# A rope tail shared out differently between VectorE and GpSimd, and minus-maxima turned by one transpose and sent as two rows

## The chip, the cores and the metric

The kernel runs on 1 core of one Trainium2 chip. The metric is the device time of one execution in microseconds; the number given for a kernel is the median of its runs. TensorE does the matrix products, VectorE, ScalarE and GpSimd do elementwise work (the profile calls them PE, DVE, ACT and POOL), and SyncE and ScalarE issue the DMA transfers. An engine executes its own list of instructions in order; engines wait for one another by semaphores.

## The reference

Two layers are computed on x of shape (2, 512, 512), so T = 1024 tokens, D = 512, everything in float32.

```
xn = layernorm(x)
x  = x + attention0(xn) + ffn0(xn)      # 32 query heads, 8 key/value heads, head size 16, rope, causal softmax, w_o
                                        # ffn: silu(xn Wg') * (xn Wu') Wd', 1792 wide, W' = W * (su @ sv), rank 4
xn = layernorm(x)
x  = x + attention1(xn) + ffn1(xn)      # 4 heads, tanh-like weights; ffn 1376 wide with rank-16 additions
```

In attention0 each query head takes 16 columns of xn @ w_qkv, is turned by the rope tables (x1 cos - x2 sin, x1 sin + x2 cos), and its scores are scaled by 1/4, masked and put through a softmax.

## The kernel before, in words

**Products in three passes.** A float32 operand is split into a rounded part "hi" (ScalarE copies it into fp32r) and the rest "lo" (a subtraction, mostly on GpSimd). `three_pass` (L50 to L54) then makes hi*hi + lo*hi + hi*lo, three matmuls of 128x512 each for one 128-row slice.

**The qkv stage** (`qkv_stage`, L449). SyncE loads the eight 128-token tiles of x (four before `w_qkv`, four after it, L489), the weights and tables. Tiles 0 to 3 are normalised (`Norm`, L64), transposed on TensorE and split. GpSimd subtracts the low halves of the weights (L521, then four chunks, L524). Six "pairs" (batch, k) of products follow in the order of `pairs` (L477): keys and two halves of the queries of batch 0, then of batch 1. For pair n, VectorE multiplies by cos and sin (L611, four instructions), GpSimd adds and subtracts into `rope_sum` (L538, L540), ScalarE makes `rope_hi` (L579), GpSimd makes `rope_lo` in `rest(n)` (L531), and SyncE stores all to DRAM (`store_pair`, L504), from where `load_stack` brings the stacked operands of a group back. In its iteration n GpSimd runs `rest(n - 1)`, and after the loop `rest(5)`. Buffers alternate with n % 2, so ScalarE waits for the store of pair n - 2 before it overwrites them. Tiles 4 to 7 are normalised meanwhile and transposed behind pairs 0 and 1.

**The attention stage** (`attention_stage`, L759) interleaves the first feed-forward layer with the attention by hand. A step is one `three_pass` of a gate or up product; 16 steps make one of 14 chunks (`Up`, L145): steps 0 to 7 work on batch 0, steps 8 to 15 on batch 1. For a chunk, VectorE combines the factor product and the raw weight (L206), ScalarE and GpSimd split it (L215, L219), ScalarE takes tanh of the gate product (L281), VectorE makes `up_gated` (L288) and `hidden` (L296). TensorE may not start step 8 before `up_gated` of batch 0. The right factors of all chunks are split in four parts at steps given by `LR0_HI_AT` (ScalarE, L920) and `LR0_LO_AT` (VectorE, L137). Every instruction of an engine stands in the order of the steps.

After every third step from 18 on stands a burst of attention work; four bursts (k = 0 to 3) make one group of 4 query heads, 16 groups in all. In a group, TensorE makes scores for the row maxima (L1003), VectorE reduces them (L949) and negates two query blocks at a time (L959), `minus_max` transposes the 128x4 result of each of the two blocks (L1011), ScalarE copies the 4x256 rows out of PSUM (L890) and issues one DMA (L896) that puts them into the last row of `q_stack`, so that the second score product (`key_scores`, L1025, one burst round later) already holds score minus maximum. Query blocks 3 and 2 ("high") are turned in burst k = 3, blocks 1 and 0 ("low") in burst k = 1 of the next group. ScalarE then takes exp (L903), GpSimd masks the diagonal blocks (L868), and `values` (L1038) at k = 0 multiplies by v once all four diagonal blocks of its group are masked. `key_scores` of the first piece waits for the high rows, the piece (0, 1), the last of burst k = 2, for the low rows.

**The down stage** (`down0_stage`, L1081, with `DownBehindUp`, L394) has 14 chunks of 12 matmuls per batch. Its VectorE loop makes, for each chunk o, `down_w_eff` (L348), `down_w_lo` (L357), and beside them the reciprocals of the softmax sums (L1231, for o = 6 to 9) and their low half (L1236). Its ScalarE loop makes `down_w_hi` three chunks ahead (L353), then `down_h_hi` two chunks ahead (L367), the split of w_o (L1190) and of the attention result (L1185). GpSimd makes `down_h_lo` (L372), and after those of batch 0 and the first two of batch 1 `att_lo` (L1172), which TensorE needs right behind chunk 13.

## Time and profile before

| | |
|---|---|
| median of 3 runs | 744.0 us (743.83 to 745.27) |
| the profiled execution | 743.73 us, of which 742.0 us are the span of the trace |
| busy in the span | TensorE 698.9 us, VectorE 413.2, ScalarE 289.4, GpSimd 246.0 |
| TensorE's mean granted clock | 0.975 of full speed |

The working is made on the profiled execution: its span and 1.7 us around it. That execution lies 0.3 us below the median. A matmul of 128x512 follows the one before it after about 0.23 us at full clock; the duration that a row prints for it is longer, since matmuls overlap. "idle before <-X" is the time for which the engine had nothing to execute before this instruction, and what ended it.

### The profile page before, as it was taken

To read this page: it belongs to the slowest core of one execution; us is meant where nothing else is said; L and a number is where in the kernel's file an instruction comes from. 1 tells how busy PE (TensorE), PEld (TensorE's weight loads), DVE (VectorE), ACT (ScalarE), POOL (GpSimd) and SP (SyncE) were. 2 spreads that over 40 slices of the span, in tenths; PEclk is the share of its full clock that TensorE was granted. 3 is DMA by queue.
4 is the path that set the end of the run, shared out by engine and by line. 5 is a ranking of instruction groups with operands and counts; after the bars stand their busy time and mean duration, and the time that the engine had idled before them with its cause. 6 is when DMAs were issued, how large, how long until landed. Compare 5 with 4: busy or idle time off the path is not lost. (4 is left out here: it accounts for less than half of the span.)

```text
span 742.0 us, 10322 instructions
## 1 busy us (share of the span) xinstructions
PE 698.9 (94%) x3718; PEld 530.4 (71%) x3718; DVE 413.2 (56%) x980; ACT 289.4 (39%) x541; POOL 246.0 (33%) x246
## 2 busy tenths in 40 slices
PE   8996999999989999999999799879999999997998
PEld 6875766666656665666677588667888888875886
DVE  7653676767766756675475550386444554535611
ACT  4214145545544534455434222263333333323321
POOL 4677122222322312221434345133232332202443
PEclk9999999999999999999999999969999999998999
DMA  9337802432231225102256200110000100102211
GB/s 289 122 110 179 209 3 71 100 80 73 70 71 47 55 41 111 42 30 72 83 167 206 89 15 1 48 58 29 29 29 30 49 37 1 41 0 86 71 57 57
DMA packets 23163, 54.88 MB, mean 74 GB/s; under 512 B 3780, under 2 KB 4136, under 8 KB 22056
## 3 DMA queue, kind: packets, MB, share of 16 engines
q1 hardware_dynamic: 22856, 54.08, 26.1%
q8 instruction: 30, 0.49, 0.3%
q14 instruction: 21, 0.17, 0.1%
q10 hardware_dynamic: 256, 0.13, 0.1%
HBM read 42.53 MB, written 11.54 MB: 73 GB/s over the span
## 5 line engine op out<-in xcount | busy, mean ns | idle before, releaser
L949 DVE CUSTOM_DVE_ANT_0 bank<-bank,mask 128x512 f32<-128x512 f32 (+3 forms) x256 | 118.4, 523 | 71.8 <-PE bank L1003 71.6
L219 POOL TENSOR_TENSOR up_w_lo<-up_w_eff,up_w_hi 128x512 fp32r<-128x512 f32 x50 | 67.2, 1352 | 120.4 <-ACT up_w_hi L215 120.4
L52 PE MATMUL bank<-x0T_hi,up_w_hi 128*128 128x512 f32 x224 | 97.4, 435 | 6.7 <-DVE up_gated L288 5.9
L372 POOL TENSOR_TENSOR down_h_lo<-hidden,down_h_hi 128x512 fp32r<-128x512 f32 x50 | 64.7, 1294 | 100.4 <-ACT down_h_hi L367 100.4
L903 ACT ACTIVATE probs<-bank 128x512 f32<-128x512 f32 x160 | 85.4, 598 | 32.1 <-PE bank L1025 29.5
L54 PE MATMUL bank<-x0T_lo,up_w_hi 128*128 128x512 f32 x224 | 90.2, 403 | 0.0
L53 PE MATMUL bank<-x0T_hi,up_w_lo 128*128 128x512 f32 x224 | 90.1, 402 | 0.0
L868 POOL TENSOR_SCALAR_AFFINE_SELECT probs<-probs 128x512 f32<-128x512 f32 x64 | 39.9, 635 | 133.3 <-ACT probs L903 133.3
L52 PE MATMUL bank<-down_w_hi,down_h_hi 128*128 128x512 f32 x200 | 79.4, 397 | 3.2 <-POOL down_h_lo L372 2.1
L53 PE MATMUL bank<-down_w_hi,down_h_lo 128*128 128x512 f32 x200 | 78.7, 394 | 0.0
L54 PE MATMUL bank<-down_w_lo,down_h_hi 128*128 128x512 f32 x200 | 78.6, 393 | 0.0
L52 PE MATMUL bank<-x1T_hi,up_w_hi 128*128 128x512 f32 x176 | 73.2, 416 | 3.6 <-DVE hidden L296 3.2
L54 PE MATMUL bank<-x1T_lo,up_w_hi 128*128 128x512 f32 x176 | 69.4, 395 | 0.0
L53 PE MATMUL bank<-x1T_hi,up_w_lo 128*128 128x512 f32 x176 | 69.4, 394 | 0.0
L52 PEld LDWEIGHTS bank<-x0T_hi,up_w_hi 128*128 128x128 f32 x224 | 42.8, 191 | 30.0 <-issue 15.5
L1025 PE MATMUL bank<-q_stack,k_stack 49*128 49x512 f32 x160 | 58.2, 447 | 5.6 <-DMA q_stack<-minus_max_rows 5.6
L367 ACT ACTIVATE down_h_hi<-hidden 128x512 fp32r<-128x512 f32 x50 | 31.5, 630 | 80.3 <-PE bank L54 76.6
L288 DVE SCALAR_TENSOR_TENSOR up_gated<-up_tanh,bank 128x512 f32<-128x512 f32 x50 | 34.2, 684 | 50.1 <-ACT up_tanh L281 50.1
L1003 PE MATMUL bank<-k_stack,q_stack 48*128 48x512 f32 (+3 forms) x256 | 57.5, 344 | 0.0
L296 DVE SCALAR_TENSOR_TENSOR hidden<-up_gated,bank 128x512 f32<-128x512 f32 x50 | 34.3, 685 | 39.0 <-PE bank L54 38.8
L215 ACT ACTIVATE up_w_hi<-up_w_eff 128x512 fp32r<-128x512 f32 x50 | 31.2, 631 | 54.4 <-DVE up_w_eff L206 54.3
L54 PEld LDWEIGHTS bank<-x0T_lo,up_w_hi 128*128 128x128 f32 x224 | 43.2, 193 | 10.6
(142 smaller groups left out, 1332.1 us busy)
## 6 DMA issues: line engine op xcount, KB each, us to landing
w_raw<-in_w_gate_up SPq DMA_DIRECT2D x25, 512.0 KB, 4.0
w_raw<-in_w_down SPq DMA_DIRECT2D x25, 256.0 KB, 2.8
q_stack<-q_hi SPq DMA_DIRECT2D x32, 128.0 KB, 4.0
att<-att_T SPq DMA_DIRECT2D x16, 256.0 KB, 2.0
x<-in_x SPq DMA_DIRECT2D x8, 256.0 KB, 5.4
q_hi<-rope_hi SPq DMA_DIRECT2D x8, 256.0 KB
q_lo<-rope_lo SPq DMA_DIRECT2D x8, 256.0 KB
q_stack<-q_lo SPq DMA_DIRECT2D x16, 128.0 KB, 4.1
```

Of the source, the lines that this page charges most:

```text
L52: pe.matmul(out, w_hi, m_hi, start=first, stop=False, skip_group_check=True)
L53: pe.matmul(out, w_lo, m_hi, start=False, stop=False, skip_group_check=True)
L54: return pe.matmul(out, w_hi, m_lo, start=False, stop=last, skip_group_check=True)
L219: pool.tensor_tensor(self.half(self.w_lo[:, o % 2], k), self.half(self.w_eff, k), f32(self.half(self.w_hi[:, o % 2], k)), ALU.subtract).th ...
L288: dve.scalar_tensor_tensor(out=self.ut[:, b, :], in0=self.th[:, b, :], scalar=1.0, in1=self.product_bank(o, b, 0)[:, :], op0=ALU.add, op1= ...
L296: dve.scalar_tensor_tensor(out=self.hid[:, o, b * S:(b + 1) * S], in0=self.ut[:, b, :], scalar=0.5, in1=self.product_bank(o, b, 1)[:, :], ...
L372: pool.tensor_tensor(self.h_lo[:, k % 2, :], self.hid[:, o, b * S:(b + 1) * S], f32(self.h_hi[:, k % 2, :]), ALU.subtract).then_inc(self.h ...
L868: pool.affine_select(out=diag, in_=diag, compare_op=ALU.is_ge, fill=0.0, base=0, pattern=[[0, REP], [1, P]], channel_multiplier=-1).then_i ...
L903: act.activation(pt[:, BLOCK_OF[KEY_PIECES[p]], :, :], narrow.bank(("keys", g, p))[:, :].rearrange("p (h s) -> p h s", h=REP), ACT.Exp).th ...
L949: dve.tensor_tensor_reduce(out=own, in0=own, in1=e.mask[:, S - w:S], scale=1.0, scalar=NEG, op0=ALU.add, op1=ALU.max, accum_out=rmax[:, i, ...
L1003: last = pe.matmul(bank[:, n * w:(n + 1) * w], qst[K, slot, h + n, i * P:(i + 1) * P], kst[K, slot, 0:w], start=(n == 0), stop=(n == nh - ...
L1025: pe.matmul(narrow.bank(("keys", g, p))[:, :], kst[K, slot, j * P:(j + 1) * P], qst[K, slot, :, i * P:(i + 1) * P], start=True, stop=True) ...
```

## The change

Three places are edited.

1. **Qkv stage.** The four second tiles of x come in one DMA. VectorE takes the statistics of tiles 4 to 7 first, then subtracts the low half of the last weight chunk (which GpSimd did), then normalises the four tiles; ScalarE's four square roots stand behind its four weight copies. `rest(3)`, `rest(4)` and `rest(5)` move from GpSimd to VectorE: behind the products of pairs 4 and 5 and behind the loop. The four parts of the right factors are split at steps 6, 8, 10, 12 (hi) and 7, 9, 11, 13 (lo), where it was 1, 6, 9, 14 and 2, 7, 10, 15.
2. **Attention stage.** `minus_max` turns two query blocks with one transpose of 128x8 to 8x128. ScalarE copies 8x128 where it copied 4x256, and issues two DMAs of four rows of 128 for each half of a group, 64 in all where there were 32. The waits of `key_scores` ask for both.
3. **Down stage.** `down_w_lo` stands behind the reciprocals and their low half. On ScalarE the first two parts of w_o are split one chunk earlier, and so are the first two parts of the attention result.

```diff
@@ -461,14 +461,14 @@
         prod = sb("rope_products", [P, 2, 4, S])
...
         cos, sin = e.cos, e.sin
-        x_loaded = [sem(f"x_loaded{t}") for t in range(NT)]
+        x_loaded = [sem(f"x_loaded{t}") for t in range(NJ)] + [sem("x_second_batch_loaded")] * NJ
         norm = Norm(nc, ctx, "norm0", x_sb, x_sb, lambda t: (x_loaded[t], 16), lambda t: e.bank[4 + (t if t < NJ else t % 2)], e.ident,
...
         lr_lo, products, stored = e.lr0_lo, e.rope_products, e.rope_stored
-        w_hi_ready, w_lo_ready = sem("wqkv_hi_ready"), sem("wqkv_lo_ready")
+        w_hi_ready, w_lo_ready, w_lo_last = sem("wqkv_hi_ready"), sem("wqkv_lo_ready"), sem("wqkv_lo_last_ready")
         v_mm, v_ones = sem("v_mm"), sem("v_ones")
@@ -485,8 +485,7 @@
                 sp.dma_start(x_sb[:, t, :], d["x"][t * P:(t + 1) * P, :]).then_inc(x_loaded[t], 16)
...
                 sp.dma_start(w_raw[:, c, :], d["w_qkv"][c * P:(c + 1) * P, :]).then_inc(w_loaded[c], 16)
-            for t in range(NJ, NT):
-                sp.dma_start(x_sb[:, t, :], d["x"][t * P:(t + 1) * P, :]).then_inc(x_loaded[t], 16)
+            sp.dma_start(x_sb[:, NJ:, :], d["x"][S:].rearrange("(t p) n -> p t n", p=P)).then_inc(x_loaded[NJ], 16)
             sp.dma_start(cos[:, :], d["cos"]).then_inc(consts, 16)
...
             sp.dma_start(lr_raw[:, :], d["lr0"]).then_inc(lr_in, 16)
@@ -519,7 +518,7 @@
                 pool.memset(e.v[:, b], 1.0).then_inc(v_ones, 1)
...
             pool.tensor_tensor(w_lo[:, :, 0:P], w_raw[:, :, 0:P], f32(w_hi[:, :, 0:P]), ALU.subtract).then_inc(w_lo_ready, 1)
-            for c in range(NC):
+            for c in range(NC - 1):
                 pool.wait_ge(w_hi_ready, c + 2)
@@ -539,7 +538,7 @@
                                    ALU.subtract).then_inc(summed, 1)
...
                                    ALU.add).then_inc(summed, 1)
-                if n >= 1:
+                if 1 <= n <= 3:
                     rest(n - 1)
...
                     pool.wait_ge(lo_ready, 2)
@@ -547,8 +546,6 @@
                 if n == 4:
...
                         up.pool_lo(pool, 0, k)
-            rest(len(pairs) - 1)
-
         def scalar(act):
...
                 for c in range(NC):
@@ -566,7 +563,8 @@
             norm.act_hi(act, 3)
...
                 act.activation(w_hi[:, c, P:], w_raw[:, c, P:], ACT.Copy).then_inc(w_hi_ready, 1)
-                norm.act_std(act, NJ + c)
+            for t in range(NJ, NT):
+                norm.act_std(act, t)
             act.wait_ge(v_ones, B)
...
                 for t in HI_BEFORE.get(n, ()):
@@ -594,12 +592,19 @@
             norm.dve_norm(dve, NJ - 1)
...
                 norm.dve_lo(dve, t)
-            norm.dve_stats(dve, NJ)
-            for t in range(NJ + 1, NT):
+            for t in range(NJ, NT):
                 norm.dve_stats(dve, t)
-                norm.dve_norm(dve, t - 1)
-            norm.dve_norm(dve, NT - 1)
+            dve.wait_ge(w_hi_ready, NC + 1)
+            dve.tensor_tensor(w_lo[:, NC - 1, P:], w_raw[:, NC - 1, P:], f32(w_hi[:, NC - 1, P:]), ALU.subtract).then_inc(w_lo_last, 1)
+            for t in range(NJ, NT):
+                norm.dve_norm(dve, t)
             dve.wait_ge(consts, 32)
+
+            def rest(n):
+                R = rows[pairs[n][1]]
+                dve.wait_ge(hi_ready, n + 1)
+                dve.wait_ge(lo_ready, n)
+                dve.tensor_tensor(rot_lo[0:R, n % 2], rot[0:R, n % 2], f32(rot_hi[0:R, n % 2]), ALU.subtract).then_inc(lo_ready, 1)
...
                 dve.wait_ge(pair_mm, n + 1)
@@ -615,9 +620,12 @@
                     norm.dve_lo(dve, t)
...
                     stack_lo(dve, e.lr0, lr_raw, slice(0, D), slice(D, LR0_FIRST), lr_hi, 1, lr_lo)
+                if n >= 4:
+                    rest(n - 1)
                 if n == 4:
...
                         up.dve_combine(dve, 0, k)
+            rest(len(pairs) - 1)
...
             pe.wait_ge(e.ident_in, 16)
@@ -633,8 +641,10 @@
                     for r in range(2):
...
                         for c in range(NC):
-                            if (n, r) == (1, 0):
+                            if (n, r) == (1, 0) and c < NC - 1:
                                 pe.wait_ge(w_lo_ready, c + 2)
+                            if (n, r) == (1, 0) and c == NC - 1:
+                                pe.wait_ge(w_lo_last, 1)
                             last = three_pass(pe, e.bank[2 * (n % 2) + r][0:rows[k], :], w_hi[:, c, c0:c0 + rows[k]],
...
                                               e.xT_lo[:, c, b * S:(b + 1) * S], c == 0, c == NC - 1)
@@ -748,7 +758,7 @@
...
 LR0_REST = [slice(LR0_FIRST + 6 * n * P, LR0_FIRST + 6 * (n + 1) * P) for n in range(4)]
-LR0_HI_AT, LR0_LO_AT = {1: 0, 6: 1, 9: 2, 14: 3}, {2: 0, 7: 1, 10: 2, 15: 3}
+LR0_HI_AT, LR0_LO_AT = {6: 0, 8: 1, 10: 2, 12: 3}, {7: 0, 9: 1, 11: 2, 13: 3}
 LRD0_PARTS = [slice(CH0 * P, CH0 * P + D)] + [slice(448 * n, 448 * (n + 1)) for n in range(4)]
...
 DOWN_FACTOR = {211: 0, 214: 1, 217: 2}
@@ -768,7 +778,7 @@
         att = sb("att_T", [P, 2, S])
...
         negm = sb("minus_max", [P, NJ, REP])
-        negrow = sb("minus_max_rows", [REP, NJ, P], F32R)
+        negrow = sb("minus_max_rows", [2 * REP, 2, P], F32R)
         lrd_raw = e.hid[0:96, 10:13, :].rearrange("p o t -> p (o t)")[:, 0:CH0 * P + D]
...
         ones = sem("k_ones")
@@ -885,16 +895,15 @@
                 r, slot = rows_of(g)
...
                 if g >= 1:
-                    act.wait_ge(neg_row[half], 16 * g)
-                both = slice(2 * half, 2 * half + 2)
-                act.activation(negrow[:, both, :],
-                               narrow.bank(("minus_max", g, half))[0:REP, 0:2 * P].rearrange("h (i s) -> h i s", i=2),
-                               ACT.Copy).then_inc(neg_copied, 1)
+                    act.wait_ge(neg_row[half], 32 * g)
+                act.activation(negrow[:, half, :], narrow.bank(("minus_max", g, half))[0:2 * REP, 0:P], ACT.Copy).then_inc(neg_copied, 1)
                 act.wait_ge(neg_copied, 2 * g + 2 - half)
...
                     act.wait_ge(s2_mm, KEYS * (g - 3))
-                act.dma_start(f32(qst[r + STK - 1:r + STK, slot, :, 2 * half * P:2 * (half + 1) * P]),
-                              f32(negrow[:, both, :])).then_inc(neg_row[half], 16)
+                for n in (1, 0):
+                    i = 2 * half + n
+                    act.dma_start(f32(qst[r + STK - 1:r + STK, slot, :, i * P:(i + 1) * P]),
+                                  f32(negrow[n * REP:(n + 1) * REP, half, :])).then_inc(neg_row[half], 16)
...
                 act.wait_ge(s2_mm, KEYS * g + p + 1)
@@ -1007,19 +1016,17 @@
             def minus_max(g, half):
...
                 narrow.free(pe, ("minus_max", g, half))
-                for i in range(2):
-                    last = pe.transpose(narrow.bank(("minus_max", g, half))[0:REP, i * P:(i + 1) * P],
-                                        negm[:, 2 * half + i, :], e.ident[:, :])
-                last.then_inc(neg_mm, 1)
+                pe.transpose(narrow.bank(("minus_max", g, half))[0:2 * REP, 0:P],
+                             negm[:, 2 * half:2 * half + 2, :].rearrange("p i h -> p (i h)"), e.ident[:, :]).then_inc(neg_mm, 1)
...
                 if p == 0:
-                    pe.wait_ge(neg_row[1], 16 * (g + 1))
+                    pe.wait_ge(neg_row[1], 32 * (g + 1))
                 if (j, i) == (0, 1):
-                    pe.wait_ge(neg_row[0], 16 * (g + 1))
+                    pe.wait_ge(neg_row[0], 32 * (g + 1))
                 narrow.free(pe, ("keys", g, p))
...
                 pe.matmul(narrow.bank(("keys", g, p))[:, :], kst[K, slot, j * P:(j + 1) * P], qst[K, slot, :, i * P:(i + 1) * P],
@@ -1200,11 +1207,17 @@
                     b = (o - 5) // 2
...
                     act.activation(rden[0:2 * HEADS, b, :], den[:, b, :], ACT.Copy).then_inc(rden_hi, 1)
+                if o == CH0 - 3:
+                    wo_half(0)
+                    wo_half(1)
                 down.act_hhi(act, (o + 2) // CH0, (o + 2) % CH0)
-                if o >= CH0 - 2:
-                    wo_half(2 * (o - CH0 + 2))
-                    wo_half(2 * (o - CH0 + 2) + 1)
-            for c in range(NC):
+                if o == CH0 - 3:
+                    att_half(0)
+                if o == CH0 - 2:
+                    wo_half(2)
+                    wo_half(3)
+                    att_half(1)
+            for c in range(2, NC):
                 att_half(c)
...
                 down.act_hhi(act, 1, o)
@@ -1223,7 +1236,6 @@
...
                 down.dve_combine(dve, o)
-                down.dve_wlo(dve, o)
                 if 6 <= o < 10:
...
                     if o == 6:
@@ -1234,6 +1246,7 @@
                     low = slice(HEADS, 2 * HEADS)
...
                     dve.tensor_tensor(rden[low, b, :], den[low, b, :], f32(rden[low, b, :]), ALU.subtract).then_inc(rden_s, 1)
+                down.dve_wlo(dve, o)
                 if o >= CH0 - 3:
```

## Rows read from the trace of the kernel before

**Rows 1.** What TensorE waited for: us in total, times, longest
```profile
PE bank L52 <- DVE up_gated L288: 5.9, 1, 5.9
PE bank L1025 <- DMA q_stack<-minus_max_rows: 5.6, 4, 1.9
...
PE bank L52 <- POOL att_lo L1172: 3.8, 1, 3.8
...
PE bank L52 <- POOL down_h_lo L372: 2.1, 3, 0.9
```

**Rows 2.** Timeline, rope tail: start us, us, engine, line, operation, idle before
```profile
56.80 1.06 ACT L579 ACTIVATE rope_hi<-rope_sum 128x1024 fp32r<-128x1024 f32 x1 [6.15 <-DMA q_lo<-rope_lo]
58.46 2.51 POOL L219 TENSOR_TENSOR up_w_lo<-up_w_eff,up_w_hi 128x512 fp32r<-128x512 f32 x2 [1.99 <-ACT up_w_hi L215]
61.02 0.51 PE L52 MATMUL bank<-x0T_hi,up_w_hi 128*128 128x512 f32 x1 [0.82 <-POOL up_w_lo L219]
63.42 4.73 POOL L531 TENSOR_TENSOR rope_lo<-rope_sum,rope_hi 128x1024 fp32r<-128x1024 f32 x2
66.32 2.65 DVE L137 TENSOR_TENSOR lr<-lr_raw,lr 32x768 fp32r<-32x768 f32 x1 [5.34 <-ACT lr L920]
73.02 0.95 DVE L137 TENSOR_TENSOR lr<-lr_raw,lr 32x768 fp32r<-32x768 f32 x1
73.04 0.79 PE L52 MATMUL bank<-x0T_hi,up_w_hi 128*128 128x512 f32 x1 [5.92 <-DVE up_gated L288]
```

**Rows 3.** Line L489's loads of x tiles 4 to 7
```profile
L489 SPq DMA_DIRECT2D x<-in_x x4: 554/568/667, 5.0 to 7.0; - x4
...
DMA to landing us min/median/max: 6.7/6.8/6.8
```

**Rows 4.** Line L100, all eight: duration ns min/median/max, first and last start
```profile
L100 DVE TENSOR_SCALAR x<-x,norm_mv,norm_rstd x8: 545/548/1918, 5.9 to 20.3; 128x512 f32<-128x512 f32 x8
```

**Rows 5.** Timeline, qkv stage, GpSimd, VectorE and TensorE
```profile
13.12 4.94 POOL L524 TENSOR_TENSOR wqkv_lo<-wqkv_raw,wqkv_hi 128x640 fp32r<-128x640 f32 x3
14.71 1.92 DVE L100 TENSOR_SCALAR x<-x,norm_mv,norm_rstd 128x512 f32<-128x512 f32 x1
18.89 1.03 PE L108 MATMUL bank<-ident,x 128*128 128x128 f32 x8
```

**Rows 6.** Windows: stretch, length, busy of PE, PEld, DVE, ACT, POOL, granted clock, DMA
```profile
73.00:76.00 3.00, 2.96 (x7) 2.38 (x8) 2.58 (x3) 0.72 (x1) 0.00 (x0) 0.50 0.58 161
```

**Rows 7.** Timeline, TensorE, one burst with a transpose pair
```profile
99.30 0.38 PE L1011 MATMUL bank<-ident,minus_max 128*4 128x128 f32 x2
99.61 0.49 PE L1003 MATMUL bank<-k_stack,q_stack 48*128 48x512 f32 x1
```

**Rows 8.** Lines of `minus_max_rows`, ScalarE: duration ns min/median/max
```profile
L890 ACT ACTIVATE minus_max_rows<-bank x32: 355/373/374, 92.9 to 350.4; 4x256 fp32r<-4x256 f32 x32
L896 ACTq DMA_DIRECT2D q_stack<-minus_max_rows x32: 580/581/1178, 93.3 to 350.8; - x32
```

**Rows 9.** Timeline, last masks of a group and its value products, groups 0 and 1
```profile
108.65 1.22 POOL L868 TENSOR_SCALAR_AFFINE_SELECT probs<-probs 128x512 f32<-128x512 f32 x2 [2.28 <-ACT probs L903]
110.20 2.36 PE L1038 MATMUL bank<-probs,v_ones 128*32 128x512 f32 x32
125.23 1.22 POOL L868 TENSOR_SCALAR_AFFINE_SELECT probs<-probs 128x512 f32<-128x512 f32 x2 [0.24 <-ACT probs L903]
126.50 2.36 PE L1038 MATMUL bank<-probs,v_ones 128*32 128x512 f32 x32
```

**Rows 10.** Timeline, TensorE, the longest of its four waits for a row transfer
```profile
219.65 0.50 PE L1025 MATMUL bank<-q_stack,k_stack 49*128 49x512 f32 x1 [1.90 <-DMA q_stack<-minus_max_rows]
```

**Rows 11.** Timeline, down stage, VectorE, TensorE, GpSimd
```profile
376.04 1.74 DVE L1231 RECIPROCAL den_or_left_factors<-den_or_left_factors 64x256 f32<-64x256 f32 x1
385.03 0.50 PE L52 MATMUL bank<-down_w_hi,down_h_hi 128*128 128x512 f32 x1 [0.72 <-POOL down_h_lo L372]
411.19 2.62 POOL L1172 TENSOR_TENSOR att_lo<-attention_or_xn,att_hi 128x512 fp32r<-128x512 f32 x2 [0.29 <-ACT att_hi L1185]
```

## Prediction

> **What bounds the kernel now.** I read TensorE's row of waits first. It has the most work, and the chain that ended last runs through its matmuls, so a microsecond counts only if TensorE idles less, executes less, or runs at a higher clock. Four of its waits lie where this change works [rows 1]: 5.9 us once for `up_gated`, 5.6 us in four waits for row transfers, 3.8 us once for `att_lo`, 2.1 us in three for `down_h_lo`. Next I read the timeline ahead of each, by engine, and last the granted clock behind the longest.
>
> **Rope tail, what it gains.** Before, GpSimd ends the sums of pair 5 at 63.4, then subtracts `rope_lo` twice, 4.73 us. VectorE wants the right factors at 66.32 and needs 2.65 us for what takes 0.95 us alone [rows 2]: it stood still until GpSimd's subtraction ended at 68.15. Behind it come the second combine, ScalarE's split, its table load, tanh, `up_gated`, and TensorE restarts at 73.04. From the end of that subtraction, 68.97, this takes 4.07 us.
>
> After: `rest(4)` waits for `rope_hi` of pair 4, which is held by the store of pair 2 until 56.80 as before, and ends at 57.86. VectorE subtracts 128x1024 then, from 57.9; by the 0.95 us for 768 elements that is 1.2 us, to 59.1. GpSimd wanted to start `up_w_lo` at 58.46. The two have just been seen not to run side by side, so it starts at 59.1, 0.6 us late, and TensorE's start at 61.02 becomes 61.6 (bounds: 0, if GpSimd is first and VectorE waits, to 1.2). Queued behind it are the sums of pair 5, at 64.1 instead of 63.4, then `rope_hi`, 1.06 us, `rest(5)` on VectorE, 1.2 us with GpSimd idle, to 66.4. Both combines follow at once, for no factor split stands between them now; the second ends 0.6 us behind the first, so at 67.0 VectorE is where it was at 68.97, and the 4.07 us give a restart at 71.0 to 71.1. Gain 2.0 us, less what comes next.
>
> **First quarter, what it costs.** The last of four loads was issued at 7.0 and landed 6.7 us later [rows 3]; queued bytes are the same, so one load lands at about 13.7, 0.8 us after VectorE wants tile 4. Four statistics of 0.8 us end at 16.9. The weight subtraction then meets GpSimd's three, which end at 18.06 (17.8 without today's mutual waits), as L100 met the first of them, 1.92 us against 0.55 [rows 4, 5]. So it runs to 18.5, tiles 4 and 5 are normalised at 19.2 and 19.9 (0.13 us of reciprocal and 0.55 each), and TensorE, which transposed both from 18.89 [rows 5], starts pair 1 some 0.6 us later. From below 0, if the subtraction slips in between two of GpSimd's; from above 1.4, if its block is 0.8 us longer. TensorE has no other wait until 60, so the 0.6 us carries through. `rest(3)` runs beside the sums of pair 4 and delays them by up to 1.2 us, hidden behind the store that lands at 56.8. SyncE's stores and stack loads come earlier, and with three issues fewer at the start so do the loads queued behind x; nobody waits for those. The split parts, moved by steps, fit in ScalarE's and VectorE's idle time before step 16 (the third takes 0.95 us of VectorE; if the cover were gone, 1 us). Net: restart 1.4 us earlier.
>
> **Clock.** Behind the 5.9 us TensorE ran at 0.50, the level of 1.2 GHz [rows 6], for a while, and some ten matmuls took 0.43 us each for 0.23: 2 us. The wait is now near 3.4 us. The one of 3.8 us [rows 1] is the nearest; behind it the half-clock stretch cost about 1.3 us. I take 1.1 us, so 0.9 us is given back; bounds 0 and 2. **Rope tail in all: -2.3 us**, between -4 and 0.
>
> **Transposes, what they gain.** Two transposes and the change of tile to the next product take 0.31 us [rows 7]; the eight transposes of x take 1.03 us with the end of the last [rows 5], so one costs 0.10 to 0.13 us, and 0.105 fits both. 32 fewer: -3.4 us, all of it TensorE's own work (bounds -3.2 and -4.1). The 8x128 copy saves ScalarE 128 elements per partition, 0.11 us of 0.37.
>
> **The second row transfer, what it costs.** ScalarE's issue takes 0.58 us [rows 8] and about 0.04 us to the next; ScalarE does nothing else in it. Queued behind are, at k = 3, the last two exps, then GpSimd's two masks, then `values`. Net of the shorter copy they come 0.51 us later. How near is this already? Of 16 groups, in six the masks end 0.33 us before the value products (109.87 and 110.20 [rows 9]), in four 0.05 us before (126.45 and 126.50), which is no slack at all, and in six over 0.5 us. The products can start 0.04 us after the mask. So six waits of 0.23 us and four of 0.5 to 0.6 us, one of which hides in a longer wait: 1.4 + 1.7 + a little for the copy's start, +3.3 us. If the short pattern issues in half the time, 0.3 us, only the four remain, with +1.0 us; I take 3.0.
>
> The rows themselves: the low half must be there at the last piece of burst k = 2, some 3.5 us after its issue, and TensorE waited already four times, up to 1.90 us [rows 10]. The second transfer leaves 0.51 us later against a TensorE that comes 0.1 us earlier. If it lands so much later, the four waits grow by 2.4 us and a few that just fitted by 1.2; if it lands with the first, because both stand behind the same bulk loads, by nothing. Middle, 1.8, and 0.7 for one more half-clock stretch. **Attention in all: -3.4 + 3.0 + 1.8 + 0.7 = +2.1 us**, between -2.4 and +6.
>
> The Trainium skill speaks against the edit: "DMA: Bandwidth & Descriptors", Rules for kernel authors, says that two transfers to disjoint partition halves serialise, since both use the same engines, and to use one. By that page the split buys nothing and its cost is at least the second issue; if the data of the second starts only when the first is done, the fourth rival below follows. No row shows two row transfers in flight.
>
> **Down stage.** VectorE's turn for chunks 6 to 9 was combine, ScalarE's split (0.7 us of waiting), `down_w_lo`, then a reciprocal of 1.74 us [rows 11]: about 3.7 us against TensorE's 3.0. With the reciprocal in the wait it is 3.0, `down_w_hi` and so `down_h_hi` behind it on ScalarE come in time, and I expect the 2.1 us in three waits to go but for 0.2. For chunk 10 VectorE now waits for the copy of the reciprocals, 1.2 us, before `down_w_lo`; three chunks of lead cover that. At the end, `att_lo` waited 0.29 us for ScalarE [rows 11]; now it follows `down_h_lo` at once. The 3.8 us become 3.5: ScalarE's `down_h_hi` still waits for TensorE's chunk 13, and GpSimd's two subtractions of 1.3 us behind it stand as before, which is most of that wait. The earlier w_o splits fall into ScalarE's idle time. **Down stage: -2.2 us**, between -2.6 and -0.8.
>
> **Sum.** 743.7 - 2.3 + 2.1 - 2.2 = 741.3; against the median of 744.0, -0.36%. What a measurement can tell from no change is 0.2%, 1.5 us.
>
> **The rivals.**
> 1. *The second issue becomes the bound* (slower). All of the 0.51 us arrives at the masks and the rows, and two more half-clock stretches follow: -3.4 + 3.3 + 3.6 + 3.2 = +6.7. Then 743.7 - 4.5 + 6.7 = 745.9. For it: four groups have no slack. Against: rows behind bulk loads may land together. It decides from an attention cost above +4.5. Chance 0.14.
> 2. *The second transfer is nearly free*: a short issue and equal landing. Attention -3.4 + 1.0 + 0.3 = -2.1, total 737.1. Against: the issue took 580 ns nearly every time. Chance 0.14.
> 3. *The rope tail gives nothing*: a block of 1.4 us at the transposes, 0.6 us at the start of step 0 and a full half-clock stretch. Tail 0, total 743.6. For it: both sit on TensorE's path. Chance 0.19.
> 4. *The second row lands a whole transfer later.* The page named above would allow it. The first row transfer fits in under 3.5 us of which some 3 us may be needed; a second behind it comes 2.5 us after its need, 16 times: 741 + 38 = 779. Chance 0.02.
>
> My forecast has 0.51, its own range 739.6 to 743.0.
>
> **Numbers.** Faster by over 1.5 us (below 742.5): 0.45 of the forecast's 0.51, rival 2, and 0.02 of rival 3: 0.61. Slower (above 745.5): 0.08 of rival 1 and rival 4: 0.10. Same: the rest, 0.29. The range runs from rival 2 to the lower part of rival 1, 737.0 to 745.3; outside stand rival 4, some 0.06 of each of rivals 1 and 2, and little else.
>
> **What would show it.** Tail: TensorE starts step 8 near 71.6; `up_w_lo` begins 0.6 us behind its ScalarE copy; a gap of 0.6 us near 19. Attention: 32 transposes; two issues of 0.6 us in a row; waits of `values` for `probs` of 0.2 and 0.6 us; row waits of over 5.6 us in total. Down stage: no wait for `down_h_lo` over 0.3 us. The forecast is wrong if the second issue is short, if the half-clock stretches fall elsewhere, or if the waits at 19 and 61 are over 2 us together.

## The result and the profile after

The changed kernel takes 750.3 us in the median of seven runs (747.8 to 752.5), against 744.0 us (740.4 to 745.9) of the kernel before on the same chip: ratio 1.0070, interval 1.0051 to 1.0089. Run again on another chip (below) it was 1.0058, 1.0032 to 1.0084. The forecast was 741.3 us, and its range ended at 745.3. The change costs 5 us where a gain of 2 to 3 was expected.

The profiled execution of the changed kernel took 747.76 us with a span of 746.0 us. TensorE's waits in it, in us in total, times, longest, beside [rows 1]:

```profile
PE bank L1032 <- DMA q_stack<-minus_max_rows: 9.4, 6, 2.6
...
PE bank L1045 <- POOL probs L878: 3.5, 10, 0.6
PE bank L52 <- POOL att_lo L1179: 3.3, 1, 3.3
...
PE bank L52 <- POOL down_h_lo L372: 2.4, 3, 1.0
...
PE bank L52 <- DVE up_gated L288: 1.7, 1, 1.7
PE bank L52 <- POOL up_w_lo L219: 1.5, 2, 1.3
```

The wait for `up_gated` fell by 4.2 us, as meant. The waits for rows grew by 3.8 us, ten waits for masked probabilities (3.5 us) are new, and `down_h_lo` is waited for as long as before, 2.4 us for 2.1, though the edit was to end these waits.

**Where the lead went.** The same TensorE instruction in two traces gives the lead of one kernel over the other at that point. In us against the kernel before (minus is earlier); the start times in the head are those of the kernel before:

| TensorE instruction | changed | only tail | only minus-maxima | only down stage | second row behind exps |
|---|---|---|---|---|---|
| 1st transposes of maxima, 92.5 | -3.6 | -3.1 | +1.0 | +0.2 | -3.5 |
| 4th, 115.4 | -3.7 | -3.1 | +0.9 | +0.2 | -3.8 |
| 7th, 138.6 | -0.7 | -3.4 | +2.8 | +0.1 | -4.3 |
| 16th, 213.1 | +0.6 | -3.4 | +3.4 | +0.2 | -5.2 |
| last, 350.0 | +1.3 | -1.4 | +3.8 | +2.1 | -11.6 |
| factor product of chunk 13, 398.1 | +2.3 | -1.4 | +3.6 | +3.2 | -11.8 |
| span, 742.0 | +4.0 | -0.9 | +4.4 | +3.0 | -11.1 |

The rope tail delivers its lead. Three us of it are gone between the 4th and the 7th transposes, mostly in two waits for low rows, 1.51 and 1.24 us, that the kernel before doesn't have, and another two by the end of attention. One such column is one execution: with the down stage's edit alone, which touches nothing of the attention, TensorE is 2.1 us late at the last transposes, and that trace has one half-clock stretch more than the kernel before. So a difference of 2 us in one column need not be the edit's effect.

**One such wait.** Timeline of the changed kernel, ScalarE, SyncE and TensorE:

```profile
111.95 0.27 ACT L899 ACTIVATE minus_max_rows<-bank 8x128 fp32r<-8x128 f32 x1 [0.91 <-PE bank L1019]
112.25 1.19 ACTq L905 DMA_DIRECT2D q_stack<-minus_max_rows  x2
113.49 1.58 ACT L912 ACTIVATE probs<-bank 128x512 f32<-128x512 f32 x3 [1.27 <-PE bank L1032]
...
109.93 0.43 SPq L840 DMA_DIRECT2D q_stack<-q_hi  x1
...
112.25 0.42 SPq L841 DMA_DIRECT2D k_stack<-k_hi  x1
...
117.56 0.49 PE L1032 MATMUL bank<-q_stack,k_stack 49*128 49x512 f32 x1 [1.51 <-DMA q_stack<-minus_max_rows]
```

The two issues take 1.19 us, and ScalarE's exps stand still behind them, 1.27 us where one issue left 0.66. Meanwhile SyncE issues the six loads of the next stack (480 KB, 109.9 to 112.7): the rows leave among them, and TensorE goes on at 117.56, 5.3 us after the first issue began and 4.7 us after the second. The two longest waits, 2.6 us each, stand where SyncE has just issued a chunk of up weights (512 KB) as well:

```profile
213.89 0.35 SPq L170 DMA_DIRECT2D w_raw<-in_w_gate_up  x1
...
214.71 1.21 ACTq L905 DMA_DIRECT2D q_stack<-minus_max_rows  x2
...
220.86 0.50 PE L1032 MATMUL bank<-q_stack,k_stack 49*128 49x512 f32 x1 [2.61 <-DMA q_stack<-minus_max_rows]
```

The kernel before issues its one low row among the same loads. Timeline of the kernel before, SyncE and ScalarE:

```profile
113.64 0.43 SPq L830 DMA_DIRECT2D q_stack<-q_hi  x1
...
116.50 0.41 SPq L831 DMA_DIRECT2D k_stack<-k_hi  x1
...
116.19 0.58 ACTq L896 DMA_DIRECT2D q_stack<-minus_max_rows  x1
```

At the longest of its waits TensorE goes on at 219.65 [rows 10], 5.4 us after the row's issue at 214.23. In the changed kernel it goes on 5.5 us after the issue of the second row (215.32 to 220.86). So a row issued 0.6 us later was there about 0.6 us later.

### The profile page after: what moved, and what is told of

Same layout as the page of the kernel before. It is cut to its first block and busy times, and to the rows that moved or that the text cites. A ratio compares the mean times of both kernels' runs of the same rounds, so it can differ in the third digit from the quotient of the medians.

```text
span 746.0 us, 10287 instructions
## 1 busy us (share of the span) xinstructions
PE 699.2 (94%) x3686; PEld 527.7 (71%) x3686; DVE 420.2 (56%) x984; ACT 285.8 (38%) x541; POOL 239.4 (32%) x242
## 5 line engine op out<-in xcount | busy, mean ns | idle before, releaser
L1012 PEld LDWEIGHTS bank<-k_stack,q_stack 48*128 48x128 f32 x256 | 36.4, 189 | 21.7 <-issue 21.0
```

Of the source, the lines that this page charges most:

```text
L1012: last = pe.matmul(bank[:, n * w:(n + 1) * w], qst[K, slot, h + n, i * P:(i + 1) * P], kst[K, slot, 0:w], start=(n == 0), stop=(n == nh - ...
```

## The experiments

Each was timed beside the kernel before on the same chip; the ratio is to that kernel, with its 95% interval. The kernel before lay at 745.4, 744.4, 745.4 and 745.4 us (medians) in the four sets, so ratios are compared, not medians across sets. A trace is one execution of several, and not always a typical one: its time is given where that matters.

### Each edit alone, and in pairs

The four runs are made of whole parts of the change's diff: the qkv stage with `LR0_HI_AT` and `LR0_LO_AT` (tail), `minus_max`, `minus_max_row` and `key_scores` (minus-maxima), the two loops of the down stage (down).

> The changed kernel with the attention edit undone: two transposes and one row transfer for each half of a group, as before. Theory (the row transfers are the loss): between the first and the last transpose pair the changed kernel lost 5.0 us on the kernel before, of which 3.8 us are longer waits for rows and 3.5 us waits for masked probabilities; all of that goes, and the attention stage keeps the 3.6 us of lead that the rope tail gives it. 744.0 - 3.6 + 2.0 (half of what the down stage lost) = 742.5 us, and the waits for rows sum to 5 to 6 us again. Rival A (the down stage and the clock are the loss, the attention edit is neutral): still 749 to 750 us. Rival B (the lead of the rope tail is eaten by the row transfers whatever their form, since TensorE meets them earlier): waits for rows at 117 and 135 us from the start stay, at some 2 us together, and the time is 745 to 746 us.

> The kernel before with the attention edit alone: one transpose of 128x8 and two row transfers for each half. Theory (the row transfers are the loss): +3.5 to +5 us, 747.5 to 749 us; waits for masked probabilities 3.5 us in some ten places, waits for rows 8 to 9.5 us. Rival A (neutral): within 1.5 us of 744.0. Rival B (lead eaten by row transfers whatever their form): without the rope tail's lead TensorE comes 3.6 us later to the rows of groups 1 and 2, so their two waits of 1.5 and 1.2 us are not there, and the edit costs 1 to 2 us: 745 to 746 us.

> The kernel before with the edit of the qkv stage alone (x in one load, last weight subtraction and the rests of pairs 3 to 5 on VectorE, split parts at steps 6 to 13). Theory: the first transpose pair of attention comes 3.6 us earlier, as in the changed kernel, and the lead is kept: 740 to 741 us. Rival A (as theory for this edit, but the half-clock stretches take back what an earlier restart gives): 743 to 744 us. Rival B (the rows eat the lead): waits for rows at 117 and 135 us, 742 to 743 us.

> The kernel before with the edit of the down stage alone (the low half of the down weights behind the reciprocals, two split parts of w_o and of the attention result one chunk earlier). Theory: VectorE's subtraction with two SBUF inputs now falls together with GpSimd's and takes 1.65 us where it took 0.69, so the waits for down_h_lo stay at 2.1 to 2.6 us and the stage costs 1 to 2 us more than before: 745 to 746 us. Rival A (the down stage holds most of the loss): 748 us or more. Rival B (the down stage's loss in the changed kernel comes from what precedes it, not from this edit): 743.5 to 744.5 us.

Since the three alone did not add up to the whole, the whole was run again, and later the two pairs that were missing.

> The changed kernel once more, unaltered, beside the kernel before. The three edits alone measured +3.3 us (minus-maxima), -2.5 us (rope tail) and +0.2 us (down stage) in ratio to the kernel before; they add to +1.0 us, where the changed kernel had +5.2 us. Theory (the two transfers eat the tail's lead: at the fourth transpose pair TensorE is 3.7 us ahead of the kernel before and at the seventh 0.7 us, where the tail alone keeps 3.4): it repeats, +4 us or more. Rival (the first comparison was drawn on a chip or in runs with more half-clock stretches): +1 to +2.5 us.

> The changed kernel with the down stage's edit undone. Theory (the tail's lead is lost to the row transfers, so these two edits do not add up): +3 to +4.5 us over the kernel before, where -2.5 and +3.3 would sum to +0.8. Rival (tail and minus-maxima add up, and it is the down stage's edit that costs more behind them): +0.8 us, within 1 us.

> The changed kernel with the rope tail's edit undone. Theory (tail and minus-maxima interact): these two add up, +3.3 + 0.2 = +3.5 us. Rival (the down stage's edit costs more behind the minus-maxima's): +6 us or more.

| Edits | ratio (interval) | median, us |
|---|---|---|
| tail | 0.9967 (0.9952 to 0.9983) | 743.0 |
| minus-maxima | 1.0045 (1.0027 to 1.0062) | 748.6 |
| down | 1.0003 (0.9988 to 1.0017) | 746.3 |
| tail, down | 0.9982 (0.9966 to 0.9998) | 743.7 |
| tail, minus-maxima | 1.0039 (1.0017 to 1.0060) | 747.5 |
| minus-maxima, down | 1.0091 (1.0057 to 1.0125) | 750.7 |
| all three, again | 1.0058 (1.0032 to 1.0084) | 748.8 |

Each edit is thus measured four times, with and without the others. Taking 1.0064 for the whole, midway between its two measurements, the minus-maxima cost 0.45, 0.72, 0.88 and 0.82%, mean 0.72%, 5.3 us; the down stage costs 0.03, 0.15, 0.46 and 0.25%, mean 0.22%, 1.7 us; the tail gains 0.33, 0.06, 0.21 and 0.27%, mean 0.22%, 1.6 us. From the intervals of the eight each mean is good to about 1 us. They sum to +5.4 us; the whole is +4.8. With the attention edit undone, the run that asks most directly whether that edit is the loss, the kernel lies 0.18% below the kernel before, 1.3 us, where 1.5 were expected. The down stage's edit alone was expected at +1 to +2 us and measured +0.2, its second rival; the tail alone was expected 3 to 4 us below the kernel before and gained 2.5. The differences between the four values of an edit are hardly larger than their intervals, so an interaction of tail and row transfers isn't shown: my theory asked for +3.5 us for minus-maxima with down, and it was +6.8 (4.2 to 9.3), which is what the rival had asked for, that the down stage's edit costs more behind the minus-maxima's. By that pair it would cost 3.4 us, by the other three 0.2 to 1.9; this rival is neither shown nor excluded. The first measurement of minus-maxima alone was the low one of four.

One reason why they scatter is seen in the two profiled executions of the same changed kernel (747.8 us, the fastest of its seven, and 750.7 us, the slowest of its seven): the last transposes of the maxima start 1.3 us behind the kernel before in one and 4.1 us in the other, with 9.4 and 8.6 us of waits for rows. The windows from 90 to 350 us (busy of PE, PEld, DVE, ACT, POOL, then granted clock, DMA share, GB/s) give 0.99 for the first and, for the second:

```profile
90.00:350.00 260.00, 248.14 (x1487) 162.03 (x1489) 171.19 (x600) 121.65 (x245) 65.94 (x82) 0.97 0.24 59
```

Windows laid closely around the stretches at 1.2 GHz give 6.7 us lost by the clock in the second and 3.4 us in the first, so 3.3 us more. Of the 2.8 us between their lags 1.3 were there at the first transposes already (-2.3 against -3.6 us), where the second trace had two half-clock stretches at the rope tail and the first had one; 1.5 arise between 90 and 350 us, 3.3 more by the clock less 1.6 of shorter waits.

### What the second transfer costs without the transposes' gain

```diff
-                act.dma_start(f32(qst[r + STK - 1:r + STK, slot, :, 2 * half * P:2 * (half + 1) * P]),
-                              f32(negrow[:, both, :])).then_inc(neg_row[half], 16)
+                for i in (2 * half + 1, 2 * half):
+                    act.dma_start(f32(qst[r + STK - 1:r + STK, slot, :, i * P:(i + 1) * P]),
+                                  f32(negrow[:, i, :])).then_inc(neg_row[half], 16)
```

> The kernel before, with its two transposes and its 4x256 copy, but each half's row sent as two transfers of four rows of 128. It does one part of the attention edit alone. By the terms of the prediction it has the 3.4 us of transposes that the attention edit saved, so it stands 3.4 us above that edit alone (748.6 us in that run, +3.3 us over the kernel before): +6.7 us, some 751 us, with ten waits for masked probabilities of together 3.5 us. Rival (one transpose in place of two gives TensorE nothing, since what it saves turns into longer waits for the rows): +3.3 us, as the attention edit alone.

Measured: 754.0 us, ratio 1.0131 (1.0105 to 1.0157), +9.8 us. Ten waits for probabilities, 3.9 us, and 7.6 us for rows. The theory had +6.7 us, the rival +3.3; it is above both, so the rival is out. Against the minus-maxima alone one transpose instead of two gains 0.86%, 6.4 us, but that was the lowest of four values for the edit. Against their mean, 5.3 us, it gains 4.5: 3.4 us for the transposes, 0.5 us for the waits for probabilities (3.9 against 3.4), and 0.6 us that is within the noise. The two traces hold 0.97 and 0.99 of granted clock between 90 and 350 us, but that doesn't explain the 6.4 us: over all executions both kernels have the same mean granted clock, 0.972, and the trace with 0.97 is the slowest of its five.

### Separate waits, and the loads behind the row

Two ways of undoing one suspected cause each in the changed kernel. Own waits:

```diff
-                if p == 0:
-                    pe.wait_ge(neg_row[1], 32 * (g + 1))
-                if (j, i) == (0, 1):
-                    pe.wait_ge(neg_row[0], 32 * (g + 1))
+                if j == 0:
+                    pe.wait_ge(neg_row[i], 16 * (g + 1))
```

> The changed kernel, with a semaphore for each of the four row transfers of a group: the first piece of query block 3 waits for its own row, and so on. The row of the higher block is issued first. Theory A (the later issue and landing of the second transfer lengthens the waits for rows): the piece (0, 1) waits only for the first transfer, so the waits for rows return from 9.4 us to 6 or 7 us, while the ten waits for probabilities stay at 3.5 us; 2 to 3 us faster than the changed kernel. Theory B (both land together behind the bulk loads of the next stack): waits for rows 9 us as before, no change.

Measured: 741.3 us, ratio 0.9960 (0.9936 to 0.9983). Waits for rows 3.5 us in three, for probabilities still 3.6 us in eleven:

```profile
PE bank L1044 <- POOL probs L878: 3.6, 11, 0.6
PE bank L1031 <- DMA q_stack<-minus_max_rows: 3.5, 3, 1.5
```

Theory A holds: what TensorE waited for was the second of the two transfers. The gain on the changed kernel of the same set is 1%, 7 us, where 2 to 3 were expected. The waits for rows fell by 5.1 us and those for probabilities grew by 0.9 (from 2.7). The trace has a granted clock of 1.00 between 90 and 350 us, but it is the fastest of twelve executions, 735.7 us with the median at 741.3; what the clock gave over all of them stands further down.

Loads behind the row, in SyncE's loop (semaphore `neg_row[0]` counts both transfers of a low half):

```diff
                 if 3 <= n + 2 < GROUPS:
+                    sp.wait_ge(neg_row[0], 32 * n)
                     load_stack(sp, n + 2)
```

> The changed kernel, with SyncE holding back the six loads of the next stack (576 KB together) until the low row of the group before has landed. In the changed kernel they are issued at 109.9 to 112.6 us and the low row at 112.3 us, and the row is waited for at 117.6 us. Theory (the row stands behind the bulk loads in the same DMA engines): the row lands in some 2.5 us, the waits for low rows (9.4 us in six) fall under 2 us, two half-clock stretches go with them, and the time falls by 6 to 9 us to 741 to 744 us. Rival A (the landing time of a small row is fixed, 5 us whatever stands ahead of it): no change. Rival B (the loads then stand in front of the high row, issued some 9 us after the low one, which is needed 3 us after its issue): waits move to the first piece, and the gain is under 2 us.

Measured: 740.6 us, ratio 0.9952 (0.9931 to 0.9974), waits for rows 3.9 us in three. (The loads are 480 KB, not the 576 of the expectation, and this trace, too, is the fastest of its ten executions, 737.1 us.) Timeline of this kernel, the pair of transfers that answers to the one at 112.25 above, and the first load, which starts when both have landed:

```profile
114.76 1.20 ACTq L906 DMA_DIRECT2D q_stack<-minus_max_rows  x2
...
117.02 0.31 SPq L840 DMA_DIRECT2D q_stack<-q_hi  x1
```

Both rows are there 2.3 us after the first issue began, where it took 5.3 us among the loads. Of rival B there is a little: one wait, 1.08 us at 111.3, is for a high row. The longest that remains, 2.48 us at 282.9, is for a low row again, issued at 276.9 between a chunk of up weights (276.1) and stack loads that SyncE came to late (277.0 to 279.4). The Trainium skill says in "DMA: Bandwidth & Descriptors", Issuing engines are not separate DMA queues, that transfers issued from ScalarE and SyncE end on the same 16 DMA engines and interleave. The traces fit that: 5.3 us among SyncE's loads against 2.3 us without them.

> The kernel before, with SyncE holding back the six loads of the next stack (480 KB) until the low row of the group before has landed. Theory (a row issued among the bulk loads lands late, in the kernel before too): of its waits for rows, 5.6 us in four, 2 to 4 us go, and one or both half-clock stretches behind them, 1.7 us each: 739 to 742 us. Rival (only the changed kernel, with its second transfer, suffers from the loads; the kernel before has slack for its one low row): waits and time as before, 743 to 745 us.

The same line (with 16 for 32) in the kernel before: 740.0 us, ratio 0.9933 (0.9913 to 0.9953). Waits for rows 3.8 us in three, where it had 5.6 [rows 1]. So the kernel before had this cost too. Its gain of 5 us is larger than the 1.8 us of waits, and its profiled execution is the slowest of its six, 742.4 us; the share of the clock stands further down.

### The second issue behind the exps

```diff
                         for p in range(*KEY_BURST[s["at"]]):
                             exp_piece(s["keys"], p)
+                    if s["high"] is not None:
+                        send_row(s["high"], 1, 0)
+                    if s["low"] is not None:
+                        send_row(s["low"], 0, 0)
```

(`send_row` issues the transfer of one block; `minus_max_row` keeps that of the higher block.)

> The rope tail and the minus-maxima edits, without the down stage's, with a semaphore for each row, and ScalarE issues the lower block's row behind the burst's exps. Theory (the ten waits for probabilities come from the second issue standing ahead of the last exps): all eleven of them, 3.6 us, go; with the down stage's 0.6 us that is 4 us below the run with own waits, some 737 us, 7 us under the kernel before. Rival (those waits come from the shifted order of TensorE, which is ahead of GpSimd's masks by the transposes it saved): half of them or more stay, and the time is 739 to 741 us.

> Rope tail and minus-maxima with a semaphore for each row; the second issue stands ahead of the exps, as in the changed kernel, and the down stage is that of the kernel before. Theory: the run with the second row behind the exps differs from this one only by the eleven waits for probabilities, 3.6 us: 737 to 738 us. Rival (the down stage's edit was most of the difference): 734 to 735 us.

Measured: 733.8 us, ratio 0.9862 (0.9836 to 0.9888), against 740.5 us and 0.9951 (0.9930 to 0.9972) with own waits and no deferral, both without the down stage's edit. The two were expected 3.6 us apart and lie 6.6 apart. No wait for probabilities is left; without deferral there were nine, 3.3 us. So the theory holds as to where these waits came from. Waits for rows are 3.9 and 3.5 us. The gain, 6.6 us, is twice the waits for probabilities that went. ScalarE in the burst that answers to the one shown above:

```profile
112.16 0.58 ACTq L909 DMA_DIRECT2D q_stack<-minus_max_rows  x1
112.78 0.60 ACT L916 ACTIVATE probs<-bank 128x512 f32<-128x512 f32 x1 [0.66 <-PE bank L1038]
112.86 0.58 ACTq L909 DMA_DIRECT2D q_stack<-minus_max_rows  x1
113.28 1.08 ACT L916 ACTIVATE probs<-bank 128x512 f32<-128x512 f32 x2
```

The issue that stands behind three exps in the program is made at 112.86, beside them: it leaves 0.09 us later than it would have ahead of them (at 112.77, one issue of 0.61 us behind 112.16) and delays none.

> As the run with the second row behind the exps, and the next stack's loads held until the low half's first row has landed. Theory: holding the loads and separate waits act on the same low rows; the last 3.5 us of waits for rows fall to under 1.5 us unless the loads now stand in front of a high row, as at 111.3 and 282.9 us in the run that held the loads. Together 735 to 737 us. Rival (the loads collide with the high rows): as without the hold, or 1 to 2 us more.

> As the run with the second row behind the exps, and of the down stage's edit only ScalarE's part (two split parts of w_o and of the attention result one chunk earlier); VectorE keeps its order. Theory (of the down stage's edit, VectorE's part loses 1.0 us between the factor products 7 and 13, and ScalarE's part gains 0.45 us at the wait for att_lo): no loss between these factor products, waits for down_h_lo 2.0 us, wait for att_lo 3.3 us, 0.5 us faster than without. Rival (the 1.0 us come from ScalarE's part, whose splits stand ahead of down_h_hi): the loss between these factor products is there, waits for down_h_lo 2.3 us.

> The version with the second row behind the exps and the stack's loads behind the low row (732.2 us), with ScalarE's part of the down stage's edit added. Theory: att_lo is waited for 0.45 us less; 731.5 to 732.5 us, not told apart from 732.2. Rival (the half-clock stretches fall otherwise): 733 to 736 us.

The loads behind the row on top: 732.2 us (735 to 737 expected), 0.9840 (0.9818 to 0.9863), waits for rows 2.4 us in two, where under 1.5 were expected. Instead of that, ScalarE's part of the down stage's edit: 735.2 us, 0.9856 (0.9833 to 0.9878), waits for `down_h_lo` 2.1 us, for `att_lo` 3.3 us, and no shift between the factor products 7 and 13 (-9.41 and -9.43 us against the kernel before). With both: **731.6 us, 0.9830 (0.9799 to 0.9861)**, the fastest version, 1.7% below the kernel before. ScalarE's part can't be told from nothing in the totals.

### How much of each difference is the clock

Each execution's mean granted clock is on record beside its span. Span times (1 - granted clock) is the time that the clock took; the mean over all executions of a kernel, less that of the kernel before in the same set, splits each difference. A single granted clock is given to 0.001, 0.7 us of an execution, so a mean of five to twelve is good to some 0.5 us. In us:

| What is compared | executions' mean span | of it clock | the rest | waits, from the traces |
|---|---|---|---|---|
| minus-maxima, mean of four ways | +5.1 | +1.6 | +3.5 | |
| down stage, mean of four ways | +1.4 | +0.5 | +0.9 | |
| rope tail, mean of four ways | -1.8 | -1.0 | -0.8 | |
| own waits, in the changed kernel | -7.4 | -2.3 | -5.0 | -4.2 |
| loads behind the row, in the changed kernel | -7.7 | -2.1 | -5.6 | -3.8 |
| loads behind the row, in the kernel before | -5.1 | -2.3 | -2.8 | -1.8 |
| second issue behind the exps | -6.8 | -3.3 | -3.5 | -2.9 |

The waits are those for rows and for probabilities, one trace against one trace. Where waits went, 28 to 49% of the gain was clock, and the rest is 0.6 to 1.8 us more than the waits.

### The down stage

In the seven traces that hold VectorE's part of the edit, TensorE loses 1.0 to 1.1 us between the factor products of chunks 7 and 13; in those without, 0.1 us at most. The run with ScalarE's part only, without this loss, shows that it is VectorE's part. VectorE and GpSimd in the changed kernel, timeline:

```profile
382.31 0.69 DVE L348 SCALAR_TENSOR_TENSOR down_w_eff<-bank,w_raw 128x512 f32<-128x512 f32 x1
382.92 1.74 DVE L1243 RECIPROCAL den_or_left_factors<-den_or_left_factors 64x256 f32<-64x256 f32 x1
384.69 0.68 DVE L1248 TENSOR_TENSOR reciprocal_stack<-den_or_left_factors,reciprocal_stack 32x512 fp32r<-32x512 f32 x1
385.40 1.65 DVE L357 TENSOR_TENSOR down_w_lo<-down_w_eff,down_w_hi 128x512 fp32r<-128x512 f32 x1
387.18 0.69 DVE L348 SCALAR_TENSOR_TENSOR down_w_eff<-bank,w_raw 128x512 f32<-128x512 f32 x1
...
384.79 1.71 POOL L372 TENSOR_TENSOR down_h_lo<-hidden,down_h_hi 128x512 fp32r<-128x512 f32 x1 [3.15 <-ACT down_h_hi L367]
...
386.55 0.50 PE L52 MATMUL bank<-down_w_hi,down_h_hi 128*128 128x512 f32 x1 [0.98 <-POOL down_h_lo L372]
```

`down_w_lo` ends at 387.05; alone it would have ended some 0.7 us after 385.40. It has two operands in SBUF, and so has GpSimd's `down_h_lo`, 384.79 to 386.50: VectorE's ends 0.55 us after GpSimd's. (GpSimd's took 1.71 us and not 1.29 since L1248, with two such operands too, was running when it came.) In the kernel before it stood right behind ScalarE's split, 382.62 to 383.31, and was done before GpSimd began at 383.70. The turn that holds it, from one `down_w_eff` to the next, took 4.4 us there and takes 4.9 us now; with 0.69 us for `down_w_lo` it would be 3.9. The Trainium skill has the rule in "SBUF — State Buffer", SBUF: two separate sides: of a VectorE operation with two SBUF inputs and a GpSimd operation that reads SBUF, the one that starts first has the port pair and the other waits it out. The trace agrees, 1.65 us for 0.69.

Only 0.3 us of the loss are longer waits for `down_h_lo`. The other 0.7 us lie in chunk 12. VectorE is late by then with the first part of the normalised attention result, and the third product of `head_rows` (L1307) stands behind that. TensorE and VectorE in the changed kernel:

```profile
397.83 0.39 PE L54 MATMUL bank<-down_w_lo,down_h_hi 128*128 128x512 f32 x1
398.31 0.49 PE L1307 MATMUL bank<-reciprocal_stack,head_rows 96*128 96x512 f32 x1
398.88 0.50 PE L52 MATMUL bank<-down_w_hi,down_h_hi 128*128 128x512 f32 x1
...
397.58 0.68 DVE L1234 TENSOR_TENSOR attention_or_xn<-attention_or_xn,bank 128x512 f32<-128x512 f32 x1
```

In the kernel before that VectorE operation had ended at 394.94, and the same three matmuls start at 396.29, 396.52 and 396.75, without a gap. No run moves `down_w_lo` clear of GpSimd and keeps it behind the reciprocal; that the edit would have gained without the collision is worked out from the turns and not measured.

## Why the prediction was wrong

The sum of the three measured terms lies 7.8 us above the forecast of 741.3 (749.1, below). Of these, 3.9 us are the down stage, 3.2 us the attention, 0.7 us the rope tail, each good to about 1 us. So two steps failed, and the down stage's is the larger by its number, if not clear of the noise.

**Rope tail: right.** Forecast -2.3 us (-4 to 0); alone -2.5 us, in the mean of four ways -1.6, within the range. TensorE starts step 8 at 71.54 (forecast 71.6), `up_w_lo` begins at 59.17 and not 58.46 (0.7 for 0.6), pair 1 starts at 20.41 and not 19.68 (0.7 for 0.6). The wait for `up_gated` is 1.7 us and not 3.4, because the half-clock stretch lies ahead of it in this trace, 62.3 to 65.5, where it lay behind the wait in [rows 6]. In the four traces with the tail's edit in which it lies behind, the wait is 3.2 us. Window of the changed kernel:

```profile
62.30:65.50 3.20, 3.20 (x8) 2.52 (x9) 0.00 (x0) 0.82 (x1) 2.35 (x2) 0.50 1.00 296
```

So TensorE comes to step 8 later itself, and part of the shorter wait is not a gain. Nor is the lead at the first transposes always 3.6 us: in the twelve traces with the edit it is 1.0 to 3.6. x in one load landed 8.8 us after its issue and not 6.7; VectorE waited 0.6 us for it, as the 0.8 of the forecast had it.

**Attention: the mechanism was named, its size was wrong.** Forecast +2.1 us (-2.4 to +6); it costs 5.3. Two terms of the sum were too small, rows and clock.

- Transposes: -3.4 us forecast. In the run with the deferred issue the lead grows from the 1st to the 16th pair by 1.65 us, the waits between them being alike (0.72 and 0.75 us), 0.11 us for each transpose saved; from the 5th on it is 0.90 us, 0.08 for each. So 2.6 to 3.5 us for 32: right.
- Probabilities: six waits of 0.23 and four of 0.5 to 0.6 us forecast, 3.0; measured 3.5 in ten, six of 0.15 to 0.18 and four of 0.61 to 0.64, and 2.7 to 3.5 in the five traces with the edit. Right, and shown by moving the issue. That its cover could be had for nothing, I didn't see.
- Rows: too small. I took the middle, 1.8 us, between landing as much later as the issue (+3.6) and landing together (0). The six traces with both transfers behind the old waits have 7.6 to 9.4 us, 2.0 to 3.8 us more than before, 2.9 in the mean: the second row lands about as much later as it is issued. I had the bulk loads down as a reason for landing together; they were the reason why a row has no slack. SyncE's issues of the stack loads lie around the low row's (113.64 to 116.50 around 116.19), as its timeline in the kernel before shows.
- Clock: too small. 0.7 us forecast for one more stretch; over all executions it is 1.6 us. The single traces don't show it: between 90 and 350 us those with both transfers under one wait hold 0.97 to 0.99, those with one transfer 0.98 to 0.99.

With 3.2 us for the probabilities (their mean) the terms give -3.4 + 3.2 + 2.9 + 1.6 = +4.3 us of the 5.3 measured; the remaining 1.0 is no more than the noise.

**Down stage: wrong in sign.** Forecast -2.2 us, between -2.6 and -0.8; it costs 1.7 (in the mean; alone 0.2). "With the reciprocal in the wait it is 3.0" is the step that failed: VectorE's turns take 4.9 and 3.9 us (382.31, 387.18, 391.09), where they took 4.4 and 3.7, since `down_w_lo`, put behind the reciprocal, meets `down_h_lo`. The 3.7 and 3.0 had also left out the low half of the reciprocals, 0.7 us in two of the turns. I had used just this exclusion for the rope tail and not for the down stage. The 2.1 us of waits for `down_h_lo` did not go but became 2.3 to 2.4, and 0.7 us at the `head_rows` product came on top. `att_lo` came as forecast, 3.3 us for 3.5. The loss of 1.0 to 1.1 us, less the 0.5 us at `att_lo`, and 0.5 us of clock make about 1 us; of the remaining 0.7 no trace shows a place, and it is within the noise.

The sum with the measured terms is 743.7 - 1.6 + 5.3 + 1.7 = 749.1, within the runs. Rival 1, at 745.9, had the right mechanism at an attention cost of 6.7 us, but beside full gains elsewhere; it got 0.14. Rival 2, a second transfer that is nearly free, is what own waits and the deferred issue together made true. Rival 4 is out: two rows landed within 2.3 us. The range ended below the result because every case in it kept the down stage's gain; a case with that gain gone and rival 1's attention cost is 748 to 750.

Open: which half-clock stretch belongs to which wait. Over all executions clock and waits go together; single executions of one kernel differ by several stretches, as the two of the changed kernel do.

## What to carry to other kernels

Before a transfer on the critical path is split or delayed, look at what the other queues issue in the same two or three us: a 2 KB row behind 480 KB of loads that nobody needs for two groups costs TensorE's time, and holding the loads back costs one line. Wait for each part of a split transfer where it is used, and put an issue that isn't urgent behind the engine's next pieces of work. And when an instruction is moved into another engine's shadow, look up which instruction of a third engine it will now meet.

## What was not expected of the hardware

- ScalarE's issue of a transfer takes 0.58 us ahead of an activation and delays it by as much; behind three queued activations it is made beside them (112.86 in 112.78 to 114.36) and costs the activations nothing.
- Two rows of 4 x 128 values, issued 0.6 us apart, had both landed 2.3 us after the first issue began with SyncE's loads held; among the loads TensorE got them after 5.3 us.
- The same kernel on the same inputs had a mean granted clock of 0.99 and 0.97 over the attention stage in two executions, 3.3 us of clock lost more in the one.
- Taking waits of TensorE away gave back clock as well: 2.1 to 3.3 us in the mean of all executions, for 1.8 to 4.2 us of waits.
